# A graph-attention layer on one core: iterations of ten tiles instead of five, and the shared tiles moved to the end

## The chip, the cores and the metric

The kernel runs on one core of a Trainium2 chip. The metric is the device time of one execution in microseconds (us). Five engines work side by side, each through its own queue in order: TensorE (PE in the profile, its weight loads PEld), VectorE (DVE), ScalarE (ACT), GpSimd (POOL) and SyncE (SP), which here only issues plain DMAs.

## What is computed

There are 6250 nodes with 96 features (4 heads of 24) and 106250 edges, sorted by their target. Cut to what matters, the reference is:

```python
q = (embeds[rows] @ qW).reshape(e, HEADS, dh)
k = (embeds[cols] @ kW).reshape(e, HEADS, dh)
v = (embeds[cols] @ vW).reshape(e, HEADS, dh)
scores = jnp.clip(jnp.einsum('ehd,ehd->eh', q, k), -10.0, 10.0)
exp_s = jnp.exp(scores)
norms = jax.ops.segment_sum(exp_s, rows, num_segments=nvar)[rows]
w = exp_s / (norms + 1e-08)
res = jax.ops.segment_sum(w[:, :, None] * v, rows, num_segments=nvar).reshape(nvar, d)
return embeds + res
```

The result of the whole is `_layernorm(x + ...)` of this, with `rows` = src and `cols` = dst.

## The kernel before

The nodes form NB = 49 blocks of 128. The edges are put into tiles of 128 edges each, such that a tile's edges belong to one block (or, for the last partly filled tiles, to one of two neighbouring blocks). There are NT = 880 tiles. First q, k and v of all nodes are made; q stays in SBUF as qt, and the k and v rows go to the table kv_table in HBM.

**The sort.** The kernel brings the edges into tiles itself, in G = 6 groups of GC = 140, 110, 130, 150, 160, 160 columns of 125 edges. Per group g > 0 it does a ranking (pieces mark, tally, pair, pay, count, base, bounds, sel, table, tree, own, choose), then units of SU = 10 columns each (71 units over the groups 1 to 5), and then lower, differ, turn, choice and pick. In a unit VectorE builds three operands of 1280 elements (lhs_1, lhs_a, lhs_b: lines 1061, 1065, 1068), ScalarE ten step vectors (line 719), and TensorE runs 20 matmuls over them (line 631), one unit later than the other two (`late`). VectorE may build lhs_1 of unit v only when TensorE has finished unit v - 2, since there are two buffers (`wait(dve, s_bin, v - 1)`). pick(g) writes dst_s (line 1103), the list of rows that GpSimd gathers for the group, and GpSimd waits for it.

**The tiles.** 880 tiles go through 176 iterations of U = 5. Software pipelining spreads a set of five over several iterations m: VectorE builds its one-hot matrix ohb at m + 2 (line 1135); TensorE turns it over into ps_t (line 674), ScalarE copies that to onehT (line 767) and ohb to oneh (line 773); TensorE gathers q by matmul with onehT (ps_q, line 648; the block of each tile is read from blk_s into a register, L423); VectorE multiplies q and the gathered k (prod, line 1146), sums per head (score, line 1166) and clips (line 1174); ScalarE takes exp (line 760); one iteration on, VectorE weighs v (wv, line 1156) and TensorE sums over the tile with oneh (ps_r, line 662); and another iteration on, VectorE adds each tile's ps_r to its block in acc (add_up, line 1127). Each addition waits for the one before (s_acc), because two tiles may have the same block. In a sorting iteration the additions stand between other long operations.

**The gathers.** GpSimd issues one indirect DMA per tile (line 508) into kv, which has R = 8 places of five tiles. A place is used again when the wv of its tiles has been computed (s_wv), with one more wait on s_res.

**The shared tiles.** Blocks 2j and 2j + 1 share one tile for what is left over of both: PAIRS = 25 such tiles. They are gathered once (25 gathers) but computed as MT = 50 tiles, once for each block, in ten iterations at the head of the last group; `gathered` and `last_use` do the bookkeeping. So there are 855 gathers for 880 tiles.

**The order of the work** is written out in PLAN, which all engines follow: per group the ranking pieces are dealt out between some iterations, then the units to the following iterations, and then come the last three iterations with lower, the pieces differ, turn, choice and pick. The last group's tiles then run in plan_last. After the last addition comes a closing stage (den, division, layer norm, stores), the same in both kernels.

## Time and profile before

| | |
|---|---|
| time, median of 3 executions | 1262.86 us (1260.61 to 1265.95) |
| the profiled execution: its span | 1256.5 us, 6.4 us under that median |
| VectorE busy | 1028.6 us, 82% |
| TensorE busy | 976.0 us, 78% |
| GpSimd busy | 866.1 us, 69% |
| ScalarE busy | 656.4 us, 52% |
| HBM traffic | 77 GB/s over the span |

Of the profiled execution its span is known (first to last instruction); the three times are device times of whole executions, and 6.4 us lie between their median and the span. Busy time counts the instruction from its start to its end, and two neighbouring instructions of one engine can overlap at their ends; the distance from start to start is read from the timeline. The profile's names for the engines are PE, PEld, DVE, ACT and POOL; a "q" behind one (DVEq) is its instruction queue.

### The profile page before, as it was taken

The numbers are of one execution on the slowest core, as the hardware profiler recorded it, in microseconds if no ns is written. First come the engines' busy times: TensorE is split into PE (matmuls) and PEld (weight loads), VectorE is DVE, ScalarE is ACT, GpSimd is POOL, SyncE is SP. The second block draws the span as 40 slices with busy tenths as digits, with TensorE's granted clock in tenths as the row PEclk, the third lists the DMA queues.
The fourth block names the chain that finished last, engine by engine and source line by source line (L and its number), as shares of the span: only waits on it lengthen the run. The fifth ranks groups of instructions, "written<-read, shape, count | busy, mean of one in ns | idle before, by whom it ended". The sixth has DMA issues, their size and how long they took to land.

```text
span 1256.5 us, 23019 instructions
## 1 busy us (share of the span) xinstructions
PE 976.0 (78%) x6512; PEld 886.1 (71%) x6513; DVE 1028.6 (82%) x3053; ACT 656.4 (52%) x1469; POOL 866.1 (69%) x887
## 2 busy tenths in 40 slices
PE   8876788678776888776898777899777788888870
PEld 6765787568755788666888666788676777777760
DVE  8999998899898999889999789999668655555557
ACT  6852693249832499422899232799424322222225
POOL 1217776767777777777777777777777777777752
PEclk9996687659885599866799775799769755555555
DMA  6202222222222222222222222222622222222222
GB/s 174 88 10 76 77 80 69 74 64 75 78 73 70 70 75 79 76 74 68 77 77 80 78 75 70 79 77 78 151 79 80 77 78 78 79 78 77 77 61 77
DMA packets 67241, 98.34 MB, mean 78 GB/s; under 512 B 33127, under 2 KB 53204, under 8 KB 67134
## 3 DMA queue, kind: packets, MB, share of 16 engines
q0 software_dynamic: 41040, 84.10, 24.7%
q1 hardware_dynamic: 26094, 12.94, 3.9%
q8 instruction: 51, 0.84, 0.3%
q14 instruction: 56, 0.46, 0.1%
HBM read 89.77 MB, written 7.22 MB: 77 GB/s over the span
## 4 chain that ended last, share of the span: by engine, by line
DVE 25%; ACT 21%; POOL 20%; PE 17%; issue 13%; DVEq 2%; DMA 1%; SPq 0%; POOLq 0%; ACTq 0%
POOL kv L508 20%; ACT steps_m L719 14%; PE ps_r L662 5%; DVE acc L1127 4%; PE ps_q L648 4%; ACT oneh L773 3%; PE ps_a L631 3%; ACT onehT L767 2%; DVE steps_m L849 2%; DVE prod L1146 2%; DVE place_m L1013 2%; DVE place_m L1017 2%; DVEq L423 2%; PE ps_r L545 1%; DMA kv<-kv_table,dst_s 1%
## 5 line engine op out<-in xcount | busy, mean ns | idle before, releaser
L508 POOL DMA_INDIRECT kv<-kv_table,dst_s x855 | 843.4, 986 | 324.0 <-issue 315.8
L648 PE MATMUL ps_q<-qt,onehT 128*128 x1760 | 321.8, 348 | 108.6 <-ACT onehT L767 97.1
L648 PEld LDWEIGHTS ps_q<-qt,onehT 128*128 128x128 f32 x1760 | 291.3, 254 | 139.5 <-issue 139.0
L662 PE MATMUL ps_r<-wv,oneh 128*128 128x100 f32 x1752 | 322.5, 350 | 70.4 <-DVE wv L1156 69.9
L662 PEld LDWEIGHTS ps_r<-wv,oneh 128*128 128x128 f32 x1752 | 295.2, 258 | 87.0 <-DVE wv L1156 82.9
L719 ACT ACTIVATE steps_m<-iota_f,pos_t 125x254 f16<-125x254 f32 (+4 forms) x794 | 312.5, 502 | 16.4 <-PE ps_b L631 8.7
L1127 DVE TENSOR_TENSOR acc<-acc,ps_r 128x100 f32 x876 | 220.6, 252 | 62.9 <-issue 24.8
L767 ACT ACTIVATE onehT<-ps_t 128x640 f32<-128x640 bf16 x176 | 124.5, 707 | 183.2 <-PE ps_t L674 176.4
L760 ACT ACTIVATE wv<-clipped 128x20 f32<-128x20 f32 x176 | 39.4, 224 | 333.9 <-DVE clipped L1174 333.6
L631 PE MATMUL ps_a<-steps_m,place_m 125*128 125x254 f16 (+4 forms) x1504 | 183.9, 279 | 29.8 <-ACT steps_m L719 29.8
L1146 DVE TENSOR_TENSOR prod<-ps_q,kv 128x480 f32<-128x480 f32 x176 | 114.7, 652 | 107.3 <-DMA kv<-kv_table,dst_s 103.8
L631 PEld LDWEIGHTS ps_a<-steps_m,place_m 125*128 125x128 f16 x1504 | 163.9, 141 | 40.2 <-ACT steps_m L719 32.2
L773 ACT ACTIVATE oneh<-ohb 128x640 f32<-128x640 bf16 x176 | 163.6, 930 | 1.3 <-PE ps_r L662 1.3
L1156 DVE TENSOR_TENSOR wv<-kv,wv 128x480 f32<-128x480 f32 x176 | 113.9, 647 | 4.1 <-issue 2.2
L1166 DVE TENSOR_REDUCE score<-prod 128x20 f32<-128x480 f32 x176 | 113.3, 644 | 0.2
L674 PE MATMUL ps_t<-ident_bf,ohb 128*128 128x128 bf16 x880 | 103.2, 265 | 7.4 <-DVE ohb L1135 7.3
L1135 DVE TENSOR_TENSOR ohb<-iota_t,loc_s 128x640 bf16<-128x640 bf16 x176 | 98.0, 557 | 0.0
L674 PEld LDWEIGHTS ps_t<-ident_bf,ohb 128*128 128x128 bf16 x880 | 89.8, 138 | 11.1 <-DVE ohb L1135 9.8
L1061 DVE TENSOR_TENSOR place_m<-iota_s,ps_b 125x1280 f16<-125x1280 f16 x71 | 57.6, 811 | 7.7 <-PE ps_a L631 7.5
L1065 DVE TENSOR_TENSOR place_m<-place_m,ps_b 125x1280 f16<-125x1280 f16 x71 | 57.6, 811 | 0.2
L1068 DVE TENSOR_TENSOR place_m<-place_m,ps_b 125x1280 f16<-125x1280 f16 x71 | 57.5, 809 | 0.0
L849 DVE TENSOR_SCALAR steps_m<-bin_u 125x160 f16<-125x160 uint16 (+4 forms) x294 | 34.6, 214 | 0.2
(208 smaller groups left out, 602.2 us busy)
## 6 DMA issues: line engine op xcount, KB each, us to landing
kv<-kv_table,dst_s POOLq DMA_INDIRECT x855
kv_table<-kv SPq DMA_DIRECT2D x7, 672.0 KB, 3.7
acc<-in_x_dram SPq DMA_DIRECT2D x6, 336.0 KB, 7.8
steps_m<-in_x_dram SPq DMA_DIRECT2D x6, 336.0 KB, 6.3
out_dram<-kv SPq DMA_DIRECT2D x6, 336.0 KB
dst_i<-in_dst_dram SPq DMA_DIRECT2D x1, 415.0 KB
src_i<-in_src_dram SPq DMA_DIRECT2D x1, 346.7 KB
acc<-in_x_dram SPq DMA_DIRECT2D x1, 288.0 KB, 4.6
```

Of the source, the lines that this page charges most:

```text
L508: nc.gpsimd.indirect_dma_start(kv[:, nm, u, :], None, kv_dram, bass.IndirectOffsetOnAxis(ap=dst_s[:, n * U + u:n * U + u + 1], axis=0)).th ...
L631: mm = nc.tensor.matmul(to[:, 0:w], lhs[:, vm, :, j], steps, start=first and j == 0 and (g == 0 or lhs is lhs_a), stop=last and j == SU - ...
L648: last = nc.tensor.matmul(ps_q[nm % 2][:, u * D:(u + 1) * D], onehT[:, nm % 2, u * P:(u + 1) * P], qt[:, bass.ds(blks[u], 1), :].rearrange ...
L662: last = nc.tensor.matmul(to, oneh[:, nm % 2, u, :], wv[:, nm % 2, u, :], start=True, stop=True)
L674: last = nc.tensor.transpose(ps_t[nm % 2][:, u * P // 2:(u + 1) * P // 2].bitcast(bf16), ohb[:, nm % 4, :, u], ident_bf[:, :])
L719: last = nc.scalar.activation(theta[:, vm, j, 0:w], iota_f[0:EP, 0:w], ACT.Sign, scale=-1.0, bias=pos_t[:, bass.ds(v * SU + j, 1)])
L767: nc.scalar.activation(onehT[:, nm % 2, :], ps_t[nm % 2][:, 0:U * P // 2].bitcast(bf16), ACT.Copy).then_inc(s_oneT, 1)
L773: nc.scalar.activation(oneh[:, nm % 2, :, :], ohb[:, nm % 4, :, :].rearrange("p n u -> p u n"), ACT.Copy).then_inc(s_onf, 1)
L1127: nc.vector.tensor_tensor(at, at, from_ps, ALU.add).then_inc(s_acc, 1)
L1146: nc.vector.tensor_tensor(prod[:, nm % 2, :].rearrange("p (u d) -> p u d", u=U), ps_q[nm % 2][:, 0:U * D].rearrange("p (u d) -> p u d", u= ...
L1156: nc.vector.tensor_tensor(wv[:, nm % 2, :, 0:D].rearrange("p u (h d) -> p u h d", h=HEADS), kv[:, km, :, D:2 * D].rearrange("p u (h d) -> ...
L1166: nc.vector.tensor_reduce(score[:, nm % 2, :], prod[:, nm % 2, :].rearrange("p (h d) -> p h d", d=DH), axis=AX.X, op=ALU.add).then_inc(s_s ...
```

## The change

1. U becomes 10 = 2 x W, with W = 5. An iteration handles ten tiles, in two halves h for what is limited by a PSUM bank: ps_t, onehT, ps_q and ps_r have one buffer for each half, where they had two whole buffers in turn. multiply, weigh, reduce, build, clip, exp and the copy to oneh are one instruction each for ten tiles. onehT is still copied in two halves of five.
2. kv has R = 4 places of ten tiles (40 tiles, as before). GpSimd's extra wait on s_res goes.
3. TensorE's order in an iteration: ps_r of m - 1 first, then ps_q of m + 1, then ps_t of m + 2. ps_q of m + 1 waits for the multiply of m.
4. The additions are for the tiles of m - 1 (before: m - 2), five behind the clip and five later, and each half reads its blocks from blk_s just before its first addition.
5. The plan has half as many iterations. A ranking iteration can have pieces inside it (`mid`), between the two halves of the additions; differ, turn and choice too. Sorting iterations carry mostly two or three units: [2,3,3,3], [3,3,3,3,3], [2,2,2,2,2,2,2,3] twice, [1,2,2,2,1,2,2,2,2]. The groups are 140, 100, 140, 160, 160, 150 columns.
6. The shared tiles are the last five iterations. Each has five gathers, one multiply, one reduce and one weigh for both blocks: the two q matmuls of a tile add up in one PSUM region. The blocks are known numbers, and five additions become one instruction (add_pairs).

There are 855 gathers and 880 tiles as before.

```diff
-    U = 5
-    R = 8
+    W = 5
+    U = 2 * W
+    R = 4
...
-    GC = [140, 110, 130, 150, 160, 160]
+    GC = [140, 100, 140, 160, 160, 150]
...
-                    if Y <= n < MB or n >= MB + 2 * PAIRS // U:
-                        pool.wait_ge(s_res, last_use(n - Y) + 1)
...
+            def tiles(m, mm, sorts, mid=()):
+                n, nm = m - 1, (mm - 1) % R
+                if there(n):
+
+                    pe.wait_ge(s_wv, n + 1)
+                    pe.wait_ge(s_onf, n + 1)
+                    for h in range(2):
+                        wait(pe, s_acc, added(n - 1, h + 1))
...
+                    wait(pe, s_prod, n - 1 if shared(n - 1) else n)
+                    for h in range(2):
+                        blks = pair_blocks(n, h) if shared(n) else blocks_of(mybir.EngineType.PE, n, h)
+                        pe.wait_ge(s_oneT, 2 * n + h + 1)
...
                 def add_up(u):
 
-                    n, nm = m - 2, (mm - 2) % R
+                    n = m - 1
+                    h, r = u // W, u % W
                     if there(n):
+                        if r == 0:
+                            blks[h] = blocks_of(mybir.EngineType.DVE, n, h)
+                            dve.wait_ge(s_res, 2 * n + h + 1)
                         wait(dve, s_acc, n * U + u)
...
+                def add_pairs(h):
+
+                    n = m - 1
+                    b = (n - NK) * U + h
+                    k = len(range(b, min(b + U, NB), 2))
+                    at = acc[:, b:b + 2 * k - 1:2, :]
...
                 multiply()
                 weigh()
...
-                add_up(0)
                 reduce()
-                add_up(1)
                 build()
                 clip()
-                add_up(2)
-                if sorts:
-                    unit(*sorts[0], between=lambda i: add_up(3 + i))
-                    for sort in sorts[1:]:
-                        unit(*sort)
-                else:
-                    add_up(3)
-                    add_up(4)
+                for u in range(W):
+                    add_up(u)
+                for piece, g in mid:
+                    piece(g)
+                behind = iter(range(W, U))
+                for sort in sorts:
+                    unit(*sort, between=lambda i: [add_up(u) for u in itertools.islice(behind, 1)])
+                for u in behind:
+                    add_up(u)
```

**VectorE, from the weighing to the first unit of a sorting iteration of group 3.** ISA on the addition's line sets its address and carries its waits. The rows of before begin behind the weighing (wv) and end with a unit's first operand (place_m):

```order
L423 TENSOR_LOAD blk_s
L1127 ISA [waits s_acc,s_res]
L1127 TENSOR_TENSOR acc<-acc,ps_r0 128x100
L1166 TENSOR_REDUCE score<-prod 128x20 [waits s_prod]
L1127 ISA [waits s_acc]
L1127 TENSOR_TENSOR acc<-acc,ps_r0 128x100
L1135 TENSOR_TENSOR ohb<-iota_t,loc_s 128x640 [waits s_onf,s_ot]
L1174 TENSOR_SCALAR clipped<-score 128x20 [waits s_score]
L1127 ISA [waits s_acc]
L1127 TENSOR_TENSOR acc<-acc,ps_r0 128x100
L1061 TENSOR_TENSOR place_m<-iota_s,ps_b 125x1280 [waits s_lhs,s_bin]
```

The same stretch in the changed kernel, from the clip on (reduce and build stand directly before it):

```order
L1196 TENSOR_SCALAR clipped<-score 128x40 [waits s_score]
L414 TENSOR_LOAD blk_s
L1124 ISA [waits s_acc,s_res]
L1124 TENSOR_TENSOR acc<-acc,ps_r0 128x100
L1124 ISA [waits s_acc]
L1124 TENSOR_TENSOR acc<-acc,ps_r0 128x100
L1124 ISA [waits s_acc]
L1124 TENSOR_TENSOR acc<-acc,ps_r0 128x100
L1124 ISA [waits s_acc]
L1124 TENSOR_TENSOR acc<-acc,ps_r0 128x100
L1124 ISA [waits s_acc]
L1124 TENSOR_TENSOR acc<-acc,ps_r0 128x100
```

Before, the reduction, the build and the clip stood between the additions, and the table was read once, behind the weighing. Now five additions follow each other behind the table's read.

**VectorE, the units behind that.** Before, one unit with the last two additions, up to the next iteration's multiply:

```order
L1061 TENSOR_TENSOR place_m<-iota_s,ps_b 125x1280 [waits s_lhs,s_bin]
L1127 ISA [waits s_acc]
L1127 TENSOR_TENSOR acc<-acc,ps_r0 128x100
L1065 TENSOR_TENSOR place_m<-place_m,ps_b 125x1280 [waits s_one_lhs]
L1127 ISA [waits s_acc]
L1127 TENSOR_TENSOR acc<-acc,ps_r0 128x100
L1068 TENSOR_TENSOR place_m<-place_m,ps_b 125x1280
L1146 TENSOR_TENSOR prod<-ps_q1,kv 128x480 [waits s_q,s_kv5]
```

In the changed kernel the second read of the table stands behind the first unit's first operand, and a second unit follows:

```order
L1058 TENSOR_TENSOR place_m<-iota_s,ps_b 125x1280 [waits s_lhs,s_bin]
L414 TENSOR_LOAD blk_s
L1124 ISA [waits s_acc,s_res]
L1124 TENSOR_TENSOR acc<-acc,ps_r1 128x100
L1062 TENSOR_TENSOR place_m<-place_m,ps_b 125x1280 [waits s_one_lhs]
L1124 ISA [waits s_acc]
L1124 TENSOR_TENSOR acc<-acc,ps_r1 128x100
L1065 TENSOR_TENSOR place_m<-place_m,ps_b 125x1280
L1058 TENSOR_TENSOR place_m<-iota_s,ps_b 125x1280 [waits s_lhs,s_bin]
L1124 ISA [waits s_acc]
L1124 TENSOR_TENSOR acc<-acc,ps_r1 128x100
L1062 TENSOR_TENSOR place_m<-place_m,ps_b 125x1280 [waits s_one_lhs]
```

Every lhs_1 (place_m from iota_s) waits for s_bin, TensorE's count of finished units; there are now two of them in one iteration.

**TensorE, a sorting iteration.** Before: ps_r, the turning over (ps_t), and one unit (four rows of L631):

```order
L662 MATMUL ps_r0<-wv,oneh 128x100 [waits s_acc,s_onf,s_wv]
L662 MATMUL ps_r0<-wv,oneh 128x100 x4
L674 MATMUL ps_t1<-ident_bf,ohb 128x128 [waits s_oneT,s_one]
L674 MATMUL ps_t1<-ident_bf,ohb 128x128 x4
L631 MATMUL ps_a<-steps_m,place_m 128x244 [waits s_lhs_a,s_theta]
L631 MATMUL ps_a<-steps_m,place_m 128x244 x9
L631 MATMUL ps_a<-steps_m,place_m 128x244 [waits s_lhs]
L631 MATMUL ps_a<-steps_m,place_m 128x244 x9
```

In the changed kernel, behind ps_r and ps_q of ten tiles: the turning over in two halves, and two units, each with its wait for ScalarE's steps (s_theta):

```order
L666 MATMUL ps_t0<-ident_bf,ohb 128x128 [waits s_oneT,s_one]
L666 MATMUL ps_t0<-ident_bf,ohb 128x128 x4
L666 MATMUL ps_t1<-ident_bf,ohb 128x128 [waits s_oneT]
L666 MATMUL ps_t1<-ident_bf,ohb 128x128 x4
L624 MATMUL ps_a<-steps_m,place_m 128x254 [waits s_lhs_a,s_theta]
L624 MATMUL ps_a<-steps_m,place_m 128x254 x9
L624 MATMUL ps_a<-steps_m,place_m 128x254 [waits s_lhs]
L624 MATMUL ps_a<-steps_m,place_m 128x254 x9
L624 MATMUL ps_a<-steps_m,place_m 128x254 [waits s_lhs_a,s_theta]
L624 MATMUL ps_a<-steps_m,place_m 128x254 x9
L624 MATMUL ps_a<-steps_m,place_m 128x254 [waits s_lhs]
L624 MATMUL ps_a<-steps_m,place_m 128x254 x9
```

The second unit's wait for s_theta now stands in the same iteration as the turning over that ScalarE's copies wait for.

## Rows read from the trace of the kernel before

**Rows 1.** The page, part 1: busy us (share of the span) xinstructions.

```profile
PE 976.0 (78%) x6512; PEld 886.1 (71%) x6513; DVE 1028.6 (82%) x3053; ACT 656.4 (52%) x1469; POOL 866.1 (69%) x887
```

**Rows 2.** The page, part 5: the costliest group, xcount | busy, mean ns | idle before.

```profile
L508 POOL DMA_INDIRECT kv<-kv_table,dst_s x855 | 843.4, 986 | 324.0 <-issue 315.8
```

**Rows 3.** The gathers' line: duration min/median/max, first and last start.

```profile
L508 POOL DMA_INDIRECT kv<-kv_table,dst_s x855: 942/949/2201, 89.1 to 1214.6; - x171
```

**Rows 4.** Who VectorE waited for, 89 to 910 us: us in total, times, longest.

```profile
DVE prod L1146 <- DMA kv<-kv_table,dst_s: 11.7, 7, 4.5
```

**Rows 5.** Windows, multiplies (L1146): us, busy (x), TensorE clock; second to sixth are sorting.

```profile
88.00:910.30 822.30, 78.64 (x122) 0.78 0.29 77
135.20:188.90 53.70, 5.17 (x8) 0.83 0.29 78
269.60:336.00 66.40, 7.11 (x11) 0.90 0.27 73
426.40:499.90 73.50, 7.74 (x12) 0.90 0.28 76
601.40:689.00 87.60, 10.33 (x16) 0.94 0.29 78
789.50:888.80 99.30, 11.05 (x18) 0.94 0.29 78
```

**Rows 6.** Timeline of VectorE, one iteration without a unit: start us, us, instruction, xcount.

```profile
952.44 0.65 DVE L1146 TENSOR_TENSOR prod<-ps_q,kv 128x480 f32<-128x480 f32 x1
953.01 0.65 DVE L1156 TENSOR_TENSOR wv<-kv,wv 128x480 f32<-128x480 f32 x1
...
953.75 0.64 DVE L1166 TENSOR_REDUCE score<-prod 128x20 f32<-128x480 f32 x1
...
954.47 0.55 DVE L1135 TENSOR_TENSOR ohb<-iota_t,loc_s 128x640 bf16<-128x640 bf16 x1
954.94 0.17 DVE L1174 TENSOR_SCALAR clipped<-score 128x20 f32<-128x20 f32 x1
955.02 1.05 DVE L1127 TENSOR_TENSOR acc<-acc,ps_r 128x100 f32 x3
955.99 0.65 DVE L1146 TENSOR_TENSOR prod<-ps_q,kv 128x480 f32<-128x480 f32 x1
```

**Rows 7.** Timeline of VectorE near the end: five additions with nothing between.

```profile
1217.93 1.85 DVE L1127 TENSOR_TENSOR acc<-acc,ps_r 128x100 f32 x5
```

**Rows 8.** Reads of the block table (blk_s) by VectorE's queue.

```profile
L423 DVEq TENSOR_LOAD <-blk_s x176: 585/1182/1198, 117.0 to 1216.1; - x176
```

**Rows 9.** Timeline of one sorting iteration, all engines.

```profile
827.00 0.74 ACT L767 ACTIVATE onehT<-ps_t 128x640 f32<-128x640 bf16 x1
...
827.59 0.99 ACT L773 ACTIVATE oneh<-ohb 128x640 f32<-128x640 bf16 x1
...
827.88 1.35 PE L648 MATMUL ps_q<-qt,onehT 128*128 x10 [0.35 <-ACT onehT L767]
828.41 4.15 ACT L719 ACTIVATE steps_m<-iota_f,pos_t 125x254 f16<-125x254 f32 x10
...
830.19 0.44 PE L674 MATMUL ps_t<-ident_bf,ohb 128*128 128x128 bf16 x5
...
830.62 2.42 PE L631 MATMUL ps_a<-steps_m,place_m 125*128 125x254 f16 x20
...
832.02 0.81 DVE L1068 TENSOR_TENSOR place_m<-place_m,ps_b 125x1280 f16<-125x1280 f16 x1
...
832.75 0.65 DVE L1146 TENSOR_TENSOR prod<-ps_q,kv 128x480 f32<-128x480 f32 x1
```

**Rows 10.** Timeline at the lower TensorE clock.

```profile
1051.70 2.45 PE L648 MATMUL ps_q<-qt,onehT 128*128 x10 [0.88 <-ACT onehT L767]
```

**Rows 11.** Windows: the last group's gathers as one stretch.

```profile
924.30:1215.70 291.40, 221.35 (x230) 0.61 0.29 78
```

**Rows 12.** The line that hands a group's rows to the gathers.

```profile
L1103 DVE TENSOR_TENSOR dst_s<-bits_a,cum_a x6: 249/304/365, 87.8 to 909.9; 128x85 int32<-128x85 int32 x1, 128x110 int32<-128x110 int32 x1, 128x125 int32<-128x125 int32 x1, 128x145 int32<-128x145 int32 x1
```

273 lines of the change are left out of this document (132 added, 141 removed).

## The prediction

> **What bounds the kernel now.** Busy shares come first [rows 1]: VectorE is highest with 82%, TensorE follows, and no engine is full. The costliest group is GpSimd's 855 gathers [rows 2]. One takes 0.949 us in the median [rows 3] and about 0.30 us pass before the next ((291.4 - 221.35) / 230 in the last group [rows 11]), so 855 of them need 855 x 1.25 = 1069 us at least. From the first start to the last end 1126.5 us pass (89.1 to 1215.6). Of the 57 us between, 843.4 - 855 x 0.949 = 32 us are gathers that took longer, which the change leaves alone; some 26 us are waits for places or for a group's rows. That is all that a faster VectorE could win.
>
> The reader is then to see what feeds the gathers. From 89 to 910 us VectorE waited 11.7 us for gathered rows [rows 4], in a stretch where its rows stand almost without a gap. So up to pick(5) at 910 us [rows 12] VectorE's own work sets the pace, with GpSimd just behind (it starts the last group at 924 us), and whatever lengthens VectorE's chain before pick(5) delays the last group. After it GpSimd alone sets the pace: 230 gathers in 291.4 us, 1.267 each [rows 11]. Then come 1256.5 - 1215.7 = 41 us without gathers.
>
> **Long instructions.** I read VectorE's cost from start to start [rows 6]: multiply 0.57, weigh and reduce about the same, build 0.47, clip 0.08, which is 2.26 us; with 1.29 us for five additions it makes the iteration of 3.55, or 7.10 for ten tiles. The clip handles 20 elements, so 0.08 is about what an instruction costs without its elements. Merging two saves only that: multiply, weigh and reduce become 0.57 + 0.49 = 1.06 each, the build 0.86, the clip 0.10, together 4.14 instead of 4.52. The gain is 0.38 us in ten tiles.
>
> The recorded durations (0.65, 0.65, 0.64, 0.55) are longer than these distances; the next multiply or weigh starts before the recorded end. The Trainium skill, "VectorE: DVE Perf Modes", The DRAIN you can't avoid, says the opposite: the next operation does not start until the pipe is empty. By it the saving would be 0.8 us in ten tiles, and the iterations up to pick(5) would be 49 us cheaper, not 23. Here the starts at 952.44 and 953.01 with a duration of 0.65 speak against it.
>
> **Additions.** Before, two of five stand between longer operations and cost 0.17 each (from the weighing at 953.01 to the reduction at 953.75 are 0.74 us, 0.57 of them the weighing's [rows 6]). Five with nothing between take 1.85 us [rows 7], (1.85 - 0.25) / 4 = 0.40 from one to the next, since each waits for the one before. In the changed order both halves stand like that when there is no unit: 4 x 0.40 each. Each half also reads the block table first. That read takes 1.18 us in the median, 0.585 at best [rows 8]; before, it ran beside multiply and weigh. The queue goes in order, so the second read starts only when the fifth addition is sent, and the sixth starts 1.2 to 1.4 us after the fifth; I take 1.3. Bounds are 0.40 (hidden) and 1.4. The first read stands behind the clip, which waits for the reduction, so it runs beside the build; 1.18 + 0.1 - 0.96 leaves 0.3 (0 to 0.6). An iteration without units is then 4.14 + 0.3 + 1.6 + 1.3 + 1.6 + 0.17 = 9.1 us for ten tiles, against 7.1. There are 27 up to pick(5) (22 with ranking, 5 with differ, turn and choice), against 55 of five tiles: 27 x 9.1 - 55 x 3.55 = **+51 us**. The ranking pieces are the same 710 columns: nothing.
>
> **Sorting iterations.** They are 34 with ten tiles: 22 with two units, 10 with three, 2 with one. Count from the start of the multiply. lhs_1 of the first unit starts at 4.14 + 0.3 + 1.6 + 0.17 = 6.2, the sixth addition at 7.5, and with 0.73 for an operand (832.02 to 832.75 [rows 9]) and 0.17 for an addition between, lhs_1 of the second unit could start at 9.3 and the iteration end at 12.0. But that lhs_1 waits until TensorE has finished the unit before the first. TensorE starts ps_r when the weighing is done, at 2.3; ps_q, ps_r and ps_t took 830.62 - 827.88 = 2.74 for five tiles at the full clock, 5.5 for ten; the unit takes 2.4: 10.2. So the iteration is 12.9 us. A third unit needs the first of this iteration to be finished by TensorE, which needs ScalarE's steps. ScalarE waits for ps_t (7.8), copies twice 0.59 and once 1.5 (0.82 for half the elements), makes five steps in 2.0, and TensorE needs 2.4: 14.9, or some 0.6 less in groups 1 and 2 with their shorter steps; with 2.7 behind it, 17. The sum is 22 x 12.9 + 10 x 17 + 2 x 10 = 474, less 10 because VectorE has one unit fewer in the last iteration of each group: 464. Before, the five sorting stretches took 53.7 + 66.4 + 73.5 + 87.6 + 99.3 = 380.5 us [rows 5]. **+84 us** (without the waits for TensorE and ScalarE +41; with the table's reads hidden too +7).
>
> **Pieces inside iterations.** count once, table three times, and turn and choice five times now stand on TensorE behind ps_t of ten tiles. At the lower clock (0.50 of full speed, which is 1.2 GHz) ps_q takes 2.45 [rows 10]; ps_r has as many matmuls of about the same width, and ps_t took 0.44 at the full clock, so I count twice 2.45 + 2.45 + 0.75, 11.3 us for ten tiles, so TensorE comes to the piece at 13.6 while VectorE is there at about 8. No row shows this wait; bounds are 0 and 5.5 in each of nine places, 0 to 50 us. At the full clock there is next to none, and the additions of the second half cover part of it for turn and choice, so I take **+20**.
>
> **Edits that cost nothing.** Two reads of the table in TensorE's queue run beside ps_r (2.45 or 1.2 us). The dropped s_res wait and four places of ten rather than eight of five hold the same 40 tiles; GpSimd, at 12.7 us for ten, is quicker than VectorE up to pick(5) and waits for rows anyway. If VectorE were the quicker one, this coarser step could cost GpSimd a few us.
>
> **The sum.** pick(5) moves from 910 to 910 + 51 + 84 + 20 = 1065 us. Behind it come 225 gathers (before 230, the shared 25 among them in both): 225 x 1.267 = 285, up to 1350. VectorE needs 9.1 us and TensorE 11.3 at the lower clock for ten tiles, both under 12.7, so GpSimd is the pace here. In the five shared iterations TensorE does the work of ten tiles for 6.3 us of gathers; that fits at the full clock (5.5), not at the lower, so the end gets 0 to 10 us longer. On the other side the last additions are two instructions. I take +2. The span is 1350 + 41 + 2 = 1393, and with the 6.4 us by which the median of the runs lies above the profiled span, 1400 us (+11%).
>
> **The rivals.**
> - VectorE alone (16%): the waits for TensorE and ScalarE are covered, the additions and reads count. 910 + 51 + 41 = 1002, and 1002 + 285 + 43 + 6 = 1336. For it: in the sorting stretches ScalarE and TensorE kept pace with VectorE. Against: they had one unit in five tiles and a whole iteration to spare.
> - The table's reads are hidden (9%): 4.14 + 1.6 + 0.4 + 1.6 + 0.17 = 7.9 for an iteration without units, +18, sorting +7: pick(5) at 935, time 1269. Against: an in-order queue behind chained additions.
> - TensorE falls to its lower clock while sorting (11%): now it idles for 2 us in each iteration, waiting for ScalarE's steps. Granted were 0.83 to 0.94 of 2.4 GHz there [rows 5], while TensorE was seldom idle. At half speed the second unit's wait ends at 2.3 + 11.3 + 3 = 16.6 instead of 10.2, 6.4 us more; in a third of 32 iterations that is 68 us: 1468.
> - Faster (4%): every VectorE instruction costs its recorded duration, merged or chained. Then ten tiles are 0.8 us cheaper, additions cost no more when chained, VectorE runs ahead by 49 us up to pick(5), and the gathers never wait: 1263 - 26 = 1237. It decides if an iteration without units takes under 7.1 us for ten tiles. It is the skill's rule above ("VectorE: DVE Perf Modes"), against which rows 6 and 7 stand.
>
> **How the numbers follow.** The forecast has 60%. Its own bounds (1.2 to 1.4 for a read, 0 to 50 for the pieces) give 1365 to 1435. 1310 to 1450 takes in the first rival and part of the third; outside lie the second, the fourth and half of the third, some 18%. A measurement can tell 0.5% from no change: faster 0.04, the same 0.03 (the second rival's lower part), slower 0.93.
>
> **What would show it.** In the changed profile: dst_s written last near 1065 us; 9 us between multiplies without units or pieces, 12.9 with two units, 17 with three; 1.3 us between the fifth and the sixth addition; multiplies 1.06 before the next start; GpSimd waiting for dst_s at each group; the gathers after the last pick still at 1.27. Additions 0.2 apart, or dst_s at 900, would prove me wrong.

## The result and the profile after

| | before | changed |
|---|---|---|
| median of the runs, us | 1261.95 | 1416.29 |
| ratio, 95% interval | | 1.123, 1.120 to 1.126 |
| profiled span, us | 1256.5 | 1414.5 |
| dst_s written last, us | 909.9 | 1069.5 |
| first gather to last gather's end, us | 1126.5 | 1279.9 |
| behind the last gather, us | 40.9 | 44.4 |

The change is slower by 12.3%. The forecast was 1400, range 1310 to 1450. One of the changed kernel's four executions took 1726.5 us, in a slow state that nothing here explains; the ratio leaves it out.

The page of the changed kernel, part 1, against [rows 1]: VectorE and TensorE have less to do than before, and the span grew by 158 us. All of it is waiting.

```profile
PE 888.9 (63%) x6502; PEld 824.8 (58%) x6503; DVE 1018.1 (72%) x2572; ACT 631.7 (45%) x1292; POOL 906.3 (64%) x887
```

Part 5 of the page, the gathers, against [rows 2]: the same 855, but 40 us more of busy time. This was not foreseen; two experiments below, e4 and e8, are about it.

```profile
L502 POOL DMA_INDIRECT kv<-kv_table,dst_s x855 | 883.5, 1033 | 437.1 <-issue 292.3
```

The line that hands a group's rows to the gathers, against [rows 12]: last written at 1069.5 us, forecast 1065.

```profile
L1100 DVE TENSOR_TENSOR dst_s<-bits_a,cum_a x6: 242/311/359, 88.9 to 1069.5; 128x80 int32<-128x80 int32 x1, 128x100 int32<-128x100 int32 x1, 128x140 int32<-128x140 int32 x1, 128x150 int32<-128x150 int32 x1
```

Windows over the five sorting stretches, the multiplies (L1164) with the granted clock of TensorE behind them, against [rows 5]. They add up to 489.2 us. The windows of [rows 5] add up to 380.5, but the fourth row's window leaves out a sorting iteration (5.4 us) and the last takes in an iteration without a unit (3.6 us); from multiply to multiply the sorting iterations of before take 382.4 us. So sorting takes 106.8 us more. The granted clock is 0.85 to 0.88 in the last three stretches, where it was 0.90 to 0.94. What is not sorting between the first and the last pick takes 980.6 - 489.2 = 491.4 us, before 822.1 - 382.4 = 439.7: 51.7 more.

```profile
127.90:191.75 63.85, 4.60 (x5) 0.86 0.27 74
285.15:372.60 87.45, 5.75 (x5) 0.90 0.20 54
481.30:593.70 112.40, 9.25 (x9) 0.85 0.26 69
709.95:822.20 112.25, 9.21 (x9) 0.85 0.26 69
938.20:1051.50 113.30, 10.34 (x10) 0.88 0.26 70
```

The last group's gathers as one stretch, against [rows 11]: 299.4 us for 225, which is 1.33 each: 1.03 for a gather and 0.30 between two, without a single longer gap. The 1.267 of before did not hold.

```profile
1070.70:1370.10 299.40, 231.12 (x225) 0.77 0.27 74
```

Who waits for whom (us in total, times, longest). The first two stand ahead of additions: one is the second read of the table, in 84 iterations, the other TensorE's ps_r. The last two are the loop of the sorting iterations.

```profile
DVE acc L1124 <- issue: 76.8, 84, 1.5
DVE acc L1124 <- PE ps_r L640: 70.7, 71, 3.6
PE ps_a L624 <- ACT steps_m L713: 81.5, 34, 2.8
DVE place_m L1058 <- PE ps_a L624: 44.5, 29, 6.0
```

Timeline of VectorE, one iteration without units (start us, us, engine, line, operation, count, idle before). The long operations follow each other at 1.06 to 1.08 us, as forecast. The additions stand in two chains; between the end of the first and the start of the second lie 1.36 us of the table's read. One iteration is 9.96 us, forecast 9.1. Ahead of the first chain VectorE waits 0.72 us for ps_r, where the forecast had 0.3 for the table's read; and the sixth addition starts 1.61 us behind the fifth, where the forecast had 1.3, at most 1.4.

```profile
1070.58 1.16 DVE L1164 TENSOR_TENSOR prod<-ps_q,kv 128x960 f32<-128x960 f32 x1 [0.73 <-DVE dst_s L1100]
1071.66 1.15 DVE L1176 TENSOR_TENSOR wv<-kv,wv 128x960 f32<-128x960 f32 x1
1072.72 1.15 DVE L1187 TENSOR_REDUCE score<-prod 128x40 f32<-128x960 f32 x1
1073.78 0.95 DVE L1143 TENSOR_TENSOR ohb<-iota_t,loc_s 128x1280 bf16<-128x1280 bf16 x1
1074.65 0.18 DVE L1196 TENSOR_SCALAR clipped<-score 128x40 f32<-128x40 f32 x1
1075.55 1.86 DVE L1124 TENSOR_TENSOR acc<-acc,ps_r 128x100 f32 x5 [0.72 <-PE ps_r L640]
1078.76 1.86 DVE L1124 TENSOR_TENSOR acc<-acc,ps_r 128x100 f32 x5 [1.36 <-issue]
1080.54 1.15 DVE L1164 TENSOR_TENSOR prod<-ps_q,kv 128x960 f32<-128x960 f32 x1
```

Timeline of one iteration with two units (752.9 to 766.6 us, 13.8 us; forecast 12.9). ScalarE copies onehT when ps_t is there, then oneh, and only then makes the steps; TensorE has done the unit left over (761.52) and waits 2.52 us for five of these steps.

```profile
756.05 2.85 PE L640 MATMUL ps_r<-wv,oneh 128*128 128x100 f32 x20
758.74 2.39 PE L655 MATMUL ps_q<-qt,onehT 128*128 x20
761.51 1.30 ACT L763 ACTIVATE onehT<-ps_t 128x640 f32<-128x640 bf16 x2 [2.84 <-PE ps_t L666]
761.52 2.37 PE L624 MATMUL ps_a<-steps_m,place_m 125*128 125x254 f16 x20
762.70 1.69 ACT L769 ACTIVATE oneh<-ohb 128x1280 f32<-128x1280 bf16 x1
763.93 0.82 DVE L1058 TENSOR_TENSOR place_m<-iota_s,ps_b 125x1280 f16<-125x1280 f16 x1 [0.97 <-PE ps_a L624]
764.29 4.07 ACT L713 ACTIVATE steps_m<-iota_f,pos_t 125x254 f16<-125x254 f32 x10
```

Windows of TensorE over that wait, the unit behind it and the ps_r behind that (us, busy and count, granted clock). The wait is followed by 3.4 us at a granted 0.63, which lies between the two levels (1.2 and 2.4 GHz), so both occur in it: the unit takes 3.6 us (752.64 to 756.05 and again from 766.42), where the one at 761.52, with no wait ahead, takes 2.4.

```profile
763.90:766.40 2.50, 0.00 (x0) 1.00 0.30 84
766.40:769.80 3.40, 3.38 (x20) 0.63 0.27 73
769.90:772.40 2.50, 2.50 (x21) 0.84 0.14 39
```

### The profile page after: what moved, and what is told of

The parts are those of the page before. It is cut to its first block, busy times and chain, and to the rows that moved or that the text cites. A ratio compares the mean times of both kernels' runs of the same rounds, so it can differ in the third digit from the quotient of the medians.

```text
span 1414.5 us, 21660 instructions
## 1 busy us (share of the span) xinstructions
PE 888.9 (63%) x6502; PEld 824.8 (58%) x6503; DVE 1018.1 (72%) x2572; ACT 631.7 (45%) x1292; POOL 906.3 (64%) x887
## 4 chain that ended last, share of the span: by engine, by line
PE 34%; DVE 27%; POOL 14%; issue 12%; ACT 10%; DVEq 3%; DMA 0%; ACTq 0%; SPq 0%; POOLq 0%
POOL kv L502 14%; PE ps_r L640 12%; PE ps_a L624 9%; PE ps_q L655 7%; ACT steps_m L713 5%; DVE acc L1124 4%; DVE prod L1164 3%; DVE wv L1176 3%; ACT oneh L769 2%; DVE steps_m L848 2%; ACT onehT L763 2%; DVE place_m L1010 2%; DVEq L414 2%; DVE place_m L1014 1%; PE ps_t L666 1%
## 5 line engine op out<-in xcount | busy, mean ns | idle before, releaser
L502 POOL DMA_INDIRECT kv<-kv_table,dst_s x855 | 883.5, 1033 | 437.1 <-issue 292.3
L655 PE MATMUL ps_q<-qt,onehT 128*128 (+1 forms) x1760 | 239.5, 296 | 15.2 <-issue 14.5
L655 PEld LDWEIGHTS ps_q<-qt,onehT 128*128 128x128 f32 x1760 | 233.4, 214 | 17.6 <-issue 17.5
L769 ACT ACTIVATE oneh<-ohb 128x1280 f32<-128x1280 bf16 x88 | 145.2, 1650 | 0.0
L1164 DVE TENSOR_TENSOR prod<-ps_q,kv 128x960 f32<-128x960 f32 x83 | 95.7, 1153 | 60.3 <-DMA kv<-kv_table,dst_s 59.0
L1176 DVE TENSOR_TENSOR wv<-kv,wv 128x960 f32<-128x960 f32 (+1 forms) x88 | 99.0, 1125 | 1.1 <-ACT wv L755 1.1
L1187 DVE TENSOR_REDUCE score<-prod 128x40 f32<-128x960 f32 (+1 forms) x88 | 98.3, 1117 | 0.2
L1058 DVE TENSOR_TENSOR place_m<-iota_s,ps_b 125x1280 f16<-125x1280 f16 x71 | 58.0, 818 | 44.8 <-PE ps_a L624 44.5
L1143 DVE TENSOR_TENSOR ohb<-iota_t,loc_s 128x1280 bf16<-128x1280 bf16 x88 | 83.5, 949 | 0.1
L666 PE MATMUL ps_t<-ident_bf,ohb 128*128 128x128 bf16 x880 | 64.0, 220 | 2.8 <-DVE ohb L1143 2.8
L848 DVE TENSOR_SCALAR steps_m<-bin_u 125x140 f16<-125x140 uint16 (+3 forms) x294 | 33.9, 207 | 0.2
```

What stands on the lines that cost most here:

```text
L502: nc.gpsimd.indirect_dma_start(kv[:, nm, u, :], None, kv_dram, bass.IndirectOffsetOnAxis(ap=dst_s[:, first + u:first + u + 1], axis=0)).th ...
L655: last = nc.tensor.matmul(to[:, u * D:(u + 1) * D], onehT[:, h, u * P:(u + 1) * P], qt[:, bass.ds(blks[u], 1), :].rearrange("p a d -> p (a ...
L666: last = nc.tensor.transpose(ps_t[h][:, u * P // 2:(u + 1) * P // 2].bitcast(bf16), ohb[:, nm, h, :, u], ident_bf[:, :])
L769: nc.scalar.activation(oneh[:, nm % 2, :, :].rearrange("p (h u) n -> p h u n", h=2), ohb[:, nm, :, :, :].rearrange("p h n u -> p h u n"), ...
L1164: nc.vector.tensor_tensor(prod[:, nm % 2, :].rearrange("p (h u d) -> p h u d", h=2, d=D), ps_q_m[:, :].rearrange("p (h c) -> p h c", h=2)[ ...
L1176: nc.vector.tensor_tensor(wv[:, nm % 2, 0:tu, 0:D].rearrange("p u (h d) -> p u h d", h=HEADS), kv[:, nm, 0:tu, D:2 * D].rearrange("p u (h ...
```

## The experiments

Twelve kernels, each timed in three rounds against the kernel before (1260.2 to 1261.6 us). "Sorting" is the time of all iterations with a unit, from multiply to multiply; "rest" is what else lies between the first and the last dst_s; "last group" is the last 225 gathers (230 where marked).

| run | median us | sorting | rest | last dst_s | last group |
|---|---|---|---|---|---|
| before | 1261.95 | 382.4 | 439.7 | 909.9 | 291.4 (x230) |
| changed | 1416.3 | 489.2 | 491.4 | 1069.5 | 299.4 |
| b1_chained | 1386.4 | 477.3 | 476.9 | 1042.2 | 301.2 (x230) |
| e1_reads_early | 1383.7 | 486.3 | 472.5 | 1047.1 | 294.1 |
| e2_steps_first | 1391.7 | 471.2 | 486.4 | 1045.2 | 298.2 |
| e3_pieces_outside | 1410.3 | 484.6 | 488.1 | 1060.9 | 297.4 |
| e4_build_split | 1405.5 | 489.1 | 492.8 | 1069.1 | 289.9 |
| e5_oneh_last | 1401.7 | 467.2 | 495.8 | 1052.5 | 297.8 |
| e6_deferred | 1380.4 | 488.9 | 462.0 | 1038.0 | 287.8 |
| e7_all | 1364.7 | 468.6 | 468.9 | 1025.2 | 287.9 |
| e8_split_all | 1416.4 | 496.5 | 495.0 | 1078.7 | 288.8 |
| e9_unit_between | 1366.2 | 461.9 | 476.3 | 1025.9 | 287.6 |
| e10_two_units | 1332.8 | 428.3 | 462.3 | 979.8 | 288.1 |
| e11_filled | 1392.1 | 467.7 | 490.5 | 1048.2 | 297.8 |

### b1_chained: one part of the change alone, in the kernel before

```diff
-                if there(m - 2):
-                    blks = blocks_of(mybir.EngineType.DVE, m - 2)
-                    dve.wait_ge(s_res, m - 2 + 1)
-                add_up(0)
                 reduce()
-                add_up(1)
                 build()
                 clip()
-                add_up(2)
+                if there(m - 2):
+                    blks = blocks_of(mybir.EngineType.DVE, m - 2)
+                    dve.wait_ge(s_res, m - 2 + 1)
+                for u in range(U):
+                    add_up(u)
```

(The calls inside and behind the unit go too.)

> The kernel before (five tiles in each iteration, as it was), where VectorE reads the block table and makes all five additions in a row behind the clip, none between the longer operations nor inside a unit. This is one part of the change alone. My theory: additions with nothing between cost 0.40 us instead of 0.17, so an iteration without a unit goes from 3.55 to about 4.3 us, 55 of them up to the last pick give 43 us; the 65 sorting ones lose the same and some 0.4 for what stood inside the unit, 65 x 1.2 = 78; the time is 1262 + 120 = 1382 (1340 to 1400). Rival 1: the sorting iterations have a cover and lose nothing: 1305. Rival 2: the place of the additions is of no weight and the loss of the change lies in the ten-tile iterations: 1262 to 1275.

Measured 1386.4, ratio 1.100 (1.098 to 1.103): 125 us of loss with five tiles in each iteration and no longer instruction, against 154 for the whole change. The timeline of an iteration without a unit shows the sum of the expectation right and its parts not. Such an iteration takes 5.01 us, not 4.3, since the read moved behind the clip too and is no longer covered (0.89 us ahead of the chain). But "rest" grew by 37 us only; sorting grew by 95 (382.4 to 477.3).

```profile
1052.08 0.65 DVE L1146 TENSOR_TENSOR prod<-ps_q,kv 128x480 f32<-128x480 f32 x1
...
1054.26 0.16 DVE L1174 TENSOR_SCALAR clipped<-score 128x20 f32<-128x20 f32 x1
1055.31 1.86 DVE L1127 TENSOR_TENSOR acc<-acc,ps_r 128x100 f32 x5 [0.89 <-issue]
1057.09 0.65 DVE L1146 TENSOR_TENSOR prod<-ps_q,kv 128x480 f32<-128x480 f32 x1
```

### e1_reads_early: the reads of the table beside multiply and weigh

```diff
                 multiply()
+                if there(m - 1):
+                    blks[0] = blocks_of(mybir.EngineType.DVE, m - 1, 0)
                 weigh()
+                if there(m - 1):
+                    blks[1] = blocks_of(mybir.EngineType.DVE, m - 1, 1)
                 reduce()
```

> The changed kernel with both reads of the block table by VectorE's queue moved forward: the first stands between multiply and weigh, the second between weigh and reduce, instead of in front of the first and of the sixth addition. Nothing else is changed. My theory: in the changed kernel the fifth and the sixth addition are about 1.4 us apart because of the second read, so an iteration without units falls from 9.8 to about 8.8 us and dst_s is written last some 27 to 35 us earlier (1035 to 1042 instead of 1069.5) if only these iterations gain, and up to 65 us earlier if the sorting iterations gain too; the time is then 1350 to 1390 us, I say 1381. Rival: TensorE and ScalarE set the pace of the iterations and the read only fills time in which VectorE would wait for them: the wait moves to the matmuls of ps_r and ps_a, and the time stays within 10 us of 1416.

Measured 1383.7, 2.7 above the figure named. Sorting is unchanged (486.3 against 489.2): iterations with two units still take 13.78 us. "Rest" falls by 19 and the last group by 5. In the timeline, 0.21 us stand between the two chains instead of 1.36, and the iteration is 8.56 us (1057.78 to 1066.34).

```profile
1057.78 1.16 DVE L1163 TENSOR_TENSOR prod<-ps_q,kv 128x960 f32<-128x960 f32 x1 [0.59 <-PE ps_q L655]
...
1062.50 1.85 DVE L1123 TENSOR_TENSOR acc<-acc,ps_r 128x100 f32 x5
1064.57 1.86 DVE L1123 TENSOR_TENSOR acc<-acc,ps_r 128x100 f32 x5 [0.21 <-DVE acc L1123]
1066.34 1.15 DVE L1163 TENSOR_TENSOR prod<-ps_q,kv 128x960 f32<-128x960 f32 x1
```

So a read ahead of the second chain costs on VectorE's own path without units, and nothing with two, where the time is lost elsewhere.

### e2_steps_first and e5_oneh_last: ScalarE's order

e2: `unit(*sorts[0])`, all ten steps, ahead of the exponential, instead of five ahead and five behind the copies. e5: the copy oneh moved behind `unit(*sorts[0], halves=(1,))`.

> The changed kernel, where ScalarE makes all ten steps of the first unit of an iteration ahead of the exponential and the copies, instead of five ahead and five behind. My theory: the loop between ScalarE and TensorE holds the sorting iterations (TensorE waited 81.5 us for the steps, VectorE 44.5 us for TensorE's unit); with steps ready earlier an iteration with two units falls from 13.8 us towards 12.5, one with three from about 19 towards 17.5, together some 30 to 45 us: 1370 to 1386. Rival 1: ScalarE only shifts its wait (the copies of the one-hots come later by the five steps), and the time stays at 1416 within 10. Rival 2: the exponential comes later by up to 2 us where it is waited for, and the 34 sorting iterations get longer: 1430 to 1480.

> The changed kernel, where ScalarE copies oneh (1.6 us) behind the second half of a unit's steps instead of ahead of it. In the changed kernel TensorE waits 2.52 us for these steps in each iteration with two units, and its clock is granted at 0.63 for the 3.4 us of the unit behind the wait and at 0.82 to 0.84 in the ps_r after it, so that the unit takes 3.6 us instead of 2.4. My theory: the wait falls to about 0.9 us, with the clock nearer full, an iteration with two units takes 12.0 to 12.4 us instead of 13.8, and one with three some 1.6 less; together 35 to 55 us: 1360 to 1380, I say 1368. Rival 1: the wait shrinks but the clock falls all the same, and the iteration is 12.8: 1388 to 1395. Rival 2: VectorE's chain holds it in any case: 1405 to 1416.

e2 measured 1391.7, 6 us above its range. The gain is in iterations with three units (17.9 to 21.1 us became 14.2 to 15.8 in the first group); those with two went from 13.8 to 14.1, against the theory: TensorE no longer waits for steps but 2.8 us for the next weigh, and ps_r behind that takes 4.1 to 4.6 us. e5 measured 1401.7, between its rivals and far from 1368. In some stretches two units took 12.5 to 12.9, in others 14.1. The wait only changed its place. That TensorE waits for ScalarE was right; that ScalarE's order alone holds the loop was wrong.

### e11_filled: the clock by itself

```diff
                 for i, sort in enumerate(sorts):
+                    if i and i == len(sorts) - 1:
+                        for _ in range(18):
+                            nc.tensor.matmul(sums_of(sort[0])[0][:, 0:TS[sort[0]] + 1], zero_h[:, 0:P],
+                                             zero_h[:, 0:TS[sort[0]] + 1], start=False, stop=False)
                     unit(*sort)
```

> The changed kernel with 18 more matmuls on TensorE (a matrix of zeros, 250 columns, added to the sums of the unit) ahead of the last unit of each iteration with two or more units. They fill about 2.1 us of the 2.52 in which TensorE waits for ScalarE's steps, and do nothing else: all waits and orders are those of the changed kernel. My theory: the lower granted clock behind that wait (0.63 in the unit, 0.82 to 0.84 in ps_r) costs 1.2 + 0.35 us in each such iteration; without it an iteration with two units takes 12.2 to 12.6 instead of 13.8, 32 iterations x 1.4 = 45, less what the matmuls themselves delay: 1375 to 1392, I say 1382. Rival 1: the clock is not what the loop costs, or other waits close up behind it: 1405 to 1418. Rival 2: the matmuls delay the unit more than they help: slower than 1418.

Measured 1392.1, ratio 1.104 (1.102 to 1.106): 24 us faster by work that does nothing. An iteration with two units takes 12.49 to 12.79 us instead of 13.8. In the timeline, and in the window of the unit shown below it, the wait for steps is 0.59 us, the unit behind takes 2.42 instead of 3.6, ps_r 2.48 instead of 2.85, and the granted clock stays at 1.00.

```profile
752.14 2.11 PE L676 MATMUL ps_a<-zero_h 128*128 128x254 f16 x18
754.84 2.42 PE L626 MATMUL ps_a<-steps_m,place_m 125*128 125x254 f16 x20 [0.59 <-ACT steps_m L719]
757.32 2.48 PE L642 MATMUL ps_r<-wv,oneh 128*128 128x100 f32 x20
```

```profile
754.85:757.25 2.40, 2.40 (x20) 1.00 0.32 84
```

The ordering and the waits are those of the changed kernel, so these 24 us belong to the clock; 21.5 of them lie in the sorting stretches (489.2 to 467.7). The Trainium skill, "TensorE: Matmul & The Clock Gate", Why this matters for your kernels, advises against idle gaps between bursts of matmuls, but names longer gaps than this one; here a gap of 2.5 us in an iteration was followed by the lower clock, and the measurement decides.

### e3_pieces_outside

```diff
-        PLAN.append(("iters", m, g, units, mid))
+        PLAN.append(("iters", m, g, units, ((), ())))
+        for name in mid[0]:
+            PLAN.append(("piece", name, mid[1]))
```

> The changed kernel with the sorting pieces that stand inside an iteration (between the two halves' additions on VectorE) put behind that iteration, at whose end all additions are made. The term of the prediction (+20 us for pieces that wait on TensorE behind ps_t of ten tiles) says 1396. What the changed kernel's trace now suggests: outside the sorting stretches it lost 49.6 us, while 27 iterations of about 9.85 us against 55 of 3.55 alone would be 71, so that pieces inside iterations seem to save some 20 us, since they cover waits; by this the time is about 1436. If where they stand does not matter, 1416 within 7.

Measured 1410.3, 6 us less than the changed kernel, and the last dst_s 9 us earlier. The intervals of the two ratios meet (1.118 to 1.122 here), so this is at the edge of what can be told. Pieces inside iterations cost under 10 us: neither the 20 of the prediction nor the gain of 20 that I had read out of the trace.

### e4_build_split and e8_split_all: what the long instructions bring and cost

e4 makes the build in two instructions, e8 multiply, weigh, reduce and build:

```diff
-                        nc.vector.tensor_tensor(ohb[:, nm, :, :, :],
-                                                iota_t[:, :, :].unsqueeze(1).to_broadcast([P, 2, P, W]),
...
+                        for h in range(2):
+                            last = nc.vector.tensor_tensor(ohb[:, nm, h, :, :], iota_t[:, :, :],
+                                                           loc_s[:, bass.ds(n * U + h * W, W)].unsqueeze(1)
+                                                           .to_broadcast([P, P, W]), ALU.is_equal)
+                        last.then_inc(s_one, 1)
```

> The changed kernel with the build (ohb, the comparison over 1280 elements) as two instructions of 640 elements each, as before the change; multiply, weigh and reduce stay long. In the last group of the changed kernel a gather takes 1.33 us instead of the 1.267 of before (299.4 us for 225), and once in each ten one lasts 1.3 to 1.8 us beside a long VectorE instruction; one that I looked at stood beside the build. If the build's length is the cause, the last group falls from 299.4 to about 287 us and the time by 10 us or more: 1400 to 1406. Rival: it is not the length of that instruction (another one, or the state of the queue of transfers): the last group stays at 295 to 303 us, the split costs 83 x 0.04 = 3 us, and the time is 1412 to 1424.

> The changed kernel with multiply, weigh, reduce and build of ten tiles as two instructions of five tiles each, the way they were before; all else as changed. This is the part of the change that was to bring something, undone. My theory, from start-to-start times: the split costs 0.08 to 0.1 us for each of four, 0.36 us in ten tiles where VectorE holds the pace, 61 x 0.36 = 22 us up to the last pick at most, and less in sorting iterations, where waits for TensorE cover it: dst_s written last 5 to 22 us later than 1069.5. In the last group it gives the gathers back their length (the build alone gave 9.5 us): 285 to 290 us instead of 299.4. Together 1405 to 1430, I say 1414. Rival (recorded durations): 2 x 0.65 instead of 1.15 and so on, 0.6 us in ten tiles: 1425 to 1440 in spite of the gathers. Second rival: the length costs the gathers more than the merging saves everywhere: below 1403.

e4 measured 1405.5 and e8 1416.4, the time of the changed kernel. The long instructions as such bring nothing in sum: undone, the last dst_s comes 9.2 us later (1078.7), and the last group is 10.6 us shorter. Here are the page's rows on the gathers, e4 and then e8:

```profile
L502 POOL DMA_INDIRECT kv<-kv_table,dst_s x855 | 854.7, 1000 | 457.3 <-issue 293.2
```

```profile
L502 POOL DMA_INDIRECT kv<-kv_table,dst_s x855 | 842.0, 985 | 478.7 <-issue 293.5
```

The gathers' busy time is 883.5 us with all four long, 854.7 with the build split, 842.0 with all split, and 843.4 before. So in this order of work merging lengthens the gathers by 41.5 us in all, 28.8 of them through the build. The size hangs on the order of the rest: the nine other versions below and above that keep all four long have 859.7 (e6) to 901.7 us (e5), all of them above the 854.7 of e4. In the last group the cost can vanish: e6, e7, e9 and e10 keep all four long there and need 288 us, as e8 does.

The trace of the changed kernel tells which operations lengthen a gather. Each gather is counted to the VectorE operation that covers most of its first 0.94 us. Beside the build 64 of 85 gathers take longer than 1.05 us (mean 1.43), beside the weighing 28 of 56 (mean 1.30); beside the multiply, as long as the weighing, none of 68, and beside additions none of 216. Build and weigh read two tensors from SBUF, the multiply reads one of its two from PSUM. This agrees with a rule of the Trainium skill, "GPSIMD Engine Reference", Key points: GpSimd shares its interfaces to SBUF with VectorE, with contention where VectorE reads two tensors from SBUF. No run changed where an operand lies, so that part is read from the trace and not tried. One such gather, from the timeline of the changed kernel, beside the build:

```profile
1195.58 0.94 DVE L1143 TENSOR_TENSOR ohb<-iota_t,loc_s 128x1280 bf16<-128x1280 bf16 x1
1195.91 1.43 POOL L502 DMA_INDIRECT kv<-kv_table,dst_s  x1 [0.30 <-issue]
```

Up to the last pick this costs little, because VectorE sets the pace and the gathers then wait less. Behind it, every such us counts.

### e6_deferred and e7_all: additions back between the long operations

Without a unit, an iteration leaves the second half's additions to the next one:

```diff
                 multiply()
+                if late:
+                    blks[1] = blocks_of(mybir.EngineType.DVE, m - 2, 1)
                 weigh()
+                if there(m - 1):
+                    blks[0] = blocks_of(mybir.EngineType.DVE, m - 1, 0)
+                add_old()
                 reduce()
+                add_old()
                 build()
+                add_old()
                 clip()
+                add_old(2)
```

e7 adds to this the reads in sorting iterations, e3, e5, and for three units e2.

> The changed kernel, where an iteration without units leaves the additions of its second half to the next iteration, and these stand between the long operations there (weigh, reduce, build, clip), with both reads of the block table beside multiply and weigh. Sorting iterations keep their order, but for the first read. My theory (long instructions are fine, what costs is the chained additions and the reads in front of them): an iteration without units takes 7.2 to 7.6 us instead of 9.8, as 7.1 for ten tiles before; 27 x 2.3 = 62 us, dst_s written last near 1007, the time 1345 to 1365, I say 1354. Rival: the next limit is TensorE at its lower clock (11.3 us for ten tiles, 9 at a granted 0.7), which now waits for the additions in the middle of an iteration: about 20 us gained, 1390 to 1400.

> All edits together on the changed kernel: additions of the second half left to the next iteration where no unit stands, reads of the block table beside multiply and weigh also in sorting iterations, the pieces behind their iterations, oneh copied behind the second half of the steps, and all ten steps first where three units stand. If the parts add up: 1416 less 62 for the additions, 45 for ScalarE's order, 25 for iterations with three units, 6 for the pieces, 7 for reads in sorting iterations: about 1271 (1255 to 1295), within 1 per cent of the kernel before: then chained additions, reads and ScalarE's order are the whole loss. Rival: the waits are the same time seen from several engines and the edits take only part of each other's gain: 1300 to 1340, and something is left that belongs to ten tiles in an iteration as such.

e6 measured 1380.4, between theory and rival and nearer to the rival. "Rest" fell by 29 us, not by 62. e7 measured 1364.7, far from 1271 and above the rival's 1340 too: the edits take only part of each other's gain. Its waits show a new one, VectorE's multiply for ps_q, but all except 2.9 us of it lies behind the last pick, where the gathers set the pace. Up to the last pick the largest is VectorE's lhs_1 for TensorE's unit (second row; 44.5 us in the changed kernel):

```profile
DVE prod L1170 <- PE ps_q L657: 62.2, 17, 4.8
DVE place_m L1061 <- PE ps_a L626: 55.6, 28, 3.6
```

In sorting iterations the loop goes through VectorE and TensorE: the second lhs_1 waits for the unit left over, which TensorE does behind ps_r, ps_q and ps_t, and ps_r waits for the weigh of the next iteration. Each closed wait let the next appear, and each leaves TensorE idle in one piece, 0.9 to 2.9 us here.

### e9_unit_between and e10_two_units: the loop cut

e9: TensorE does the unit left over between ps_r and ps_q; ScalarE makes the first unit's ten steps behind the exponential. e10: the same only with two units, and oneh copied ahead of onehT:

```diff
                         last.then_inc(s_res, 1)
+                first = sorts[:1] if now[0] == 2 else []
+                for sort in first:
+                    unit(*sort)
                 n, nm = m + 1, (mm + 1) % R
...
+                if two:
+                    unit(*sorts[0])
+                    copy_oneh(m + 1, mm)
```

> The kernel with all edits of the run before it (1364.7 us), where in iterations with two or more units TensorE does the unit left over from the iteration before between ps_r and ps_q, instead of behind ps_t, and ScalarE makes all ten steps of the first unit right behind the exponential. In the kernel with all edits the sorting iterations still take 12.5 to 14.1 us for two units: VectorE's second lhs_1 waits 1.4 to 2.9 us for TensorE's unit, which stands behind ps_r, ps_q and ps_t, and ps_r waits 1.65 us for VectorE's weigh, behind which the clock is at its lower level for a part of ps_r. My theory: this loop through both engines is the rest of the sorting loss; with the unit earlier VectorE's own 11.3 us remain, 22 x 1.9 = 42 us: 1310 to 1335, I say 1322. Rival 1: ScalarE (11.25 us of work in 11.3) holds instead, or the exponential and the steps come late: 1345 to 1365. Rival 2: ps_r and the oneh copies are late because of it and the additions wait: slower than 1365.

> The kernel with all edits (1364.7 us), where only iterations with two units are ordered anew: TensorE does the unit left over from the iteration before between ps_r and ps_q, and ScalarE makes the exponential, all ten steps of the first unit, the copy oneh, the copies onehT and then the steps of the second unit. In the run before (1366.2 us) such iterations took 11.2 us as long as nobody waited, but mostly 13.55: TensorE waited 2.0 us for the second unit's steps, which stood behind both copies, and did the unit at a lower clock in 4.05 us; and iterations with three units lost 14 us in the first two groups, where the order is now as with all edits. My theory: with oneh copied in ScalarE's idle 2.6 us the steps come 1.6 us sooner, the loop is broken, and two units take 11.3 to 11.6 us instead of 13.3: 22 x 1.8 = 40 us, 1325 (1312 to 1342). Rival: ScalarE (11.25 us of work) and TensorE still catch each other, 12.5 or more: 1345 to 1366.

e9 measured 1366.2, no gain, 1 us above the range of the rival on ScalarE; its mechanism is what the trace shows. TensorE's timeline has the unit waiting for steps that stand behind both copies, and the unit itself at a lower clock:

```profile
525.45 4.06 PE L626 MATMUL ps_a<-steps_m,place_m 125*128 125x254 f16 x20 [2.02 <-ACT steps_m L718]
529.34 2.37 PE L660 MATMUL ps_q<-qt,onehT 128*128 x20
```

e10 measured 1332.8, ratio 1.057 (1.055 to 1.059), within its range of 1312 to 1342 and the best of the ten-tile kernels. In this stretch TensorE has no wait for steps left, and an iteration with two units takes 11.15 us, against 2 x 5.28 for two iterations of five tiles with one unit each before:

```profile
701.99 2.48 PE L645 MATMUL ps_r<-wv,oneh 128*128 128x100 f32 x20 [1.15 <-DVE wv L1195]
704.30 2.38 PE L629 MATMUL ps_a<-steps_m,place_m 125*128 125x254 f16 x20
706.52 2.37 PE L663 MATMUL ps_q<-qt,onehT 128*128 x20
```

Sorting is down to 428.3 us, 40.3 below e7, which is the 40 that the expectation named, and 45.9 above the kernel before. "Rest" is 462.3, 6.6 below e7 and 22.6 above before. The last pick so comes 69.9 us later than before (979.8 against 909.9).

The page's row on e10's gathers:

```profile
L507 POOL DMA_INDIRECT kv<-kv_table,dst_s x855 | 873.7, 1022 | 355.8 <-issue 296.4
```

From the first gather to the end of the last are 90.5 to 1279.0 = 1188.5 us, before 1126.5. Of the 62 us, 30.3 are longer gathers (873.7 against 843.4), 31.7 are time between them. The end behind the last gather is 51.5 us instead of 40.9. Together 72.6, all of the difference to the kernel before (1332.8 - 1260.5 = 72.3). GpSimd's waits for VectorE (a place or a group's rows) are 59.4 us, before 6.0; 53 of them lie before 569 us, in the first groups. From there to the last pick they are 6.1, and at the last pick GpSimd has eight gathers of the group before still to do. So in that later part GpSimd is near its own pace, and the long instructions should now cost rather than bring; e10 with the operations split was not run, and no version here beats the kernel before.

## Why the prediction was right, and where not

The time was 16 us above the forecast and within its range; the terms of the sum stand as follows.

**What bounds the kernel: right.** VectorE's chain up to the last pick decides, then the gathers. pick(5) came at 1069.5 us for 1065, the end took 44.4 for 43.

**Long instructions: right on VectorE, a term missing.** Undoing them moved the last dst_s by 9.2 us (multiply to clip 4.37 us against 4.07, so 0.30 in ten tiles; 0.38 forecast). The rival that every instruction costs its recorded duration is out: starts are 1.06 apart at durations of 1.15. The section of the Trainium skill that the prediction cites for it, "VectorE: DVE Perf Modes", The DRAIN you can't avoid, has an exception that the prediction left out, namely that an operation which is not held starts earlier; these starts fit the exception. What "which the change leaves alone" denied is that merging makes the gathers longer, by 40 us in all. "225 x 1.267 = 285" failed by 14 us: the window shows 299.4, and 288.8 with the operations split; but also 287.8 with all four long and additions between them (e6), so the length costs these 11 us only in the order of the changed kernel.

**Additions and reads, +51, and pieces, +20: the time outside sorting grew by 51.7, not 71, and by errors that cancel.** An iteration without units takes 9.8 to 10.0 us, not 9.1; 27 x 0.8 is 21 us more. The waits for the pieces, "+20", were 6 to 9 (e3). And 27 x 9.9 - 55 x 3.55 = 72 plus 6 is 78, which is 26 too much. The trace of before has the difference: outside sorting VectorE waited 36 us there (9 ahead of additions, 16 ahead of pieces, 10 ahead of the tiles' operations), and 55 x 3.55 leaves these waits out. In the changed kernel they are 82 us, 57 of them ahead of additions. VectorE's work apart from waits hardly changed: merging took 17 us off the tiles' operations outside sorting, and chained additions put 20 on. The mechanism itself is shown twice: b1 puts the chained additions and the uncovered read into the kernel before and gets 125 us of loss, e1 takes the reads out of the way and gets 33 us back. These are not shares of 154, since the two act through the same waits.

**Sorting, +84: 489.2 us measured, where the sum said 464.** The step that failed is the clock in "5.5 for ten; the unit takes 2.4: 10.2", which takes TensorE at its full clock. The loop was right: with the waits filled (e11) two units take 12.5 to 12.8 us where the sum said 12.9. In the changed kernel they took 13.8, since TensorE's idle time now comes in one piece. The third rival had this, at 11%, but with the size and place wrong: not 6.4 us in a third of the iterations but some 1.2 in 16 of the 25 in which VectorE has two units, 24 us in all. Iterations with three units on VectorE, all in the first two groups, took 16.8 to 21.1 (17 forecast); one unit 10.8 to 10.95 (10 forecast). In the third and the fourth sorting stretch the second iteration took 16.6 us with two units: TensorE comes to the unit left over after 4.7 us of idle time and needs 4.4 us for it.

**Whether it could have been mended.** e10 shows that most of the loss while sorting was no property of ten tiles: with the reads, pieces and additions of e7 and an order on TensorE and ScalarE that suits two units in one iteration, 61 of the 106.8 us are gone, 40 of them by the last step. VectorE's last pick still comes 70 us later than before; the gathers are 30 us longer and the end 11.

## What to carry to other kernels

When two iterations become one, their dependences are fewer but each wait is longer: look for what stood between two dependent operations and covered a latency, here additions between long operations and a table read beside a multiply, and for which engine now idles in one piece. An engine order that was balanced for one unit in each iteration has to be made again for two; in a loop through three engines, mending the order of one engine (15 and 25 us here) left most of the loss, and only orders that fit each other took the waits out (another 32 us from e7 to e10). Longer instructions on one engine are not free for the others: compare the busy time of every engine, the one untouched by the edit too.

## What was not expected of the hardware

- The gathers' total grows from 842.0 to 883.5 us when VectorE's four operations handle ten tiles in place of five, with the same elements in all; the build alone makes 28.8 of it. Beside the build 64 of 85 gathers take longer than 1.05 us, beside the multiply none of 68.
- A wait of 2.5 us on TensorE is followed by 3.4 us at a granted 0.63; 18 matmuls on zeros in its place keep the clock at 1.00 and make the kernel 24 us faster.
- Five additions to the same array, each waiting for the one before, take 1.86 us, in ten-tile and five-tile iterations alike; with one other operation between, 0.17 each [rows 6].
